# Sums written into the chain's operand and seeded into PSUM, in a fused network with three recurrences

## The reference, cut to what matters

```python
h = tanh(x_t @ Wx + h @ Wh + b)                     # stage 1, "rnn"
# then a selective state-space stage (mamba)
fused = sigmoid(concat([x_t, h]) @ w_W + w_b)       # stage 3, "gru"
hidden, output = split(fused, 2)
m = x_t @ wx_W + wx_b + hidden * (h @ wh_W + wh_b)
h = output * h + (1 - output) * tanh(m)
# then a feed-forward and a gated linear attention stage
a = x_t @ Wx + b + h @ Wh                           # stage 6, "lstm"
i, f, o, g = sigmoid, sigmoid, sigmoid, tanh of the quarters of a
c = f * c + i * g;  h = o * tanh(c)
# then a mixture of experts
```

## Time and profile before

| | |
|---|---|
| three runs | 8898.45, 8900.65, 8903.1 us; median 8900.65 |
| profiled execution | 8898.33 us, its span 8896.5 us |
| busy in the span | PE 70%, DVE 85%, ACT 48%, POOL 15% |
| rnn, from about 240 to 5419 us | DVE 4979.54 us busy of 5179 |
| GRU, about 7552 to 7952 us | DVE 143.17 us busy of 400 |
| LSTM, about 8258 to 8631 us | DVE 108.83 us busy of 373 |

### The profile page before, as it was taken

The page is one execution under the profiler, slowest core; times in us unless marked ns, Lnnn a source line. Parts: engine busy times, 40 slices in busy tenths (PEclk is TensorE's granted clock), DMA queues, the critical chain, the costliest instruction groups (busy, mean ns, idle before and its releaser), DMA issues. The chain is left out here.

```text
span 8896.5 us, 108600 instructions
## 1 busy us (share of the span) xinstructions
PE 6269.1 (70%) x33921; PEld 2486.1 (28%) x34193; DVE 7600.0 (85%) x12570; ACT 4291.4 (48%) x4428; POOL 1329.7 (15%) x1111
## 2 busy tenths in 40 slices
PE   5677777676767676767676764488888887662779
PEld 1222222222222222222222221122222222331443
DVE  5999999999999999999999996899999997336223
ACT  3666666665656665656665663233333332112222
POOL 0000000000000000000000000377777774000000
PEclk8888888888888888888888887799999999995999
DMA  0000000000000000000000000000000000000000
GB/s 6 1 1 1 1 1 1 1 1 1 1 1 1 1 1 1 1 1 1 1 1 1 1 1 22 17 3 4 4 4 4 4 4 3 0 6 3 3 14 5
DMA packets 14002, 27.97 MB, mean 3 GB/s; under 512 B 3665, under 2 KB 11602, under 8 KB 12434
## 3 DMA queue, kind: packets, MB, share of 16 engines
q1 hardware_dynamic: 13586, 22.47, 0.9%
HBM read 15.12 MB, written 7.34 MB: 3 GB/s over the span
## 5 line engine op out<-in xcount | busy, mean ns | idle before, releaser
L901 POOL TENSOR_TENSOR hc<-hh,cg 128x512 f32<-128x512 f32 x1024 | 1296.2, 1268 | 506.9 <-DVE hh L884 506.9
L829 ACT ACTIVATE ps_m<-ps_m,aneg 128x508 f32<-128x508 f32 x1024 | 673.4, 658 | 1188.6 <-DVE hh L884 1063.5
L884 DVE TENSOR_TENSOR_SCAN hh<-ps_m,bx 128x512 f32<-128x512 f32 x1024 | 1232.9, 1209 | 0.0
L800 PE MATMUL ps_m<-hc,pick 128*128 128x512 f32 x2048 | 1051.1, 597 | 2.1 <-POOL hc L901 0.8
L508 DVE TENSOR_TENSOR_SCAN co<-rx_d 128x772 f32<-128x772 f32 x544 | 915.4, 1745 | 0.0
L508 DVE TENSOR_TENSOR_SCAN co<-rh_d 128x3088 f32<-128x3088 f32 x128 | 843.8, 6592 | 31.8 <-ACT rh_d L366 28.6
L263 PE MATMUL r_ps<-rh_diag,whq 32*128 32x512 bf16 x3072 | 360.1, 624 | 666.9 <-DVE rh_diag L127 611.5
L866 DVE TENSOR_TENSOR bx<-ps_m,bg 128x512 f32<-128x512 f32 x1024 | 675.3, 664 | 45.9 <-PE ps_m L813 45.8
L439 POOL TENSOR_TENSOR r_gate<-ident 128x1 f32<-128x1 f32 x16 | 5.7, 356 | 4576.1 <-PE r_ps L255 4576.1
L255 PE MATMUL r_ps<-wdiag,xsp 32*128 32x512 bf16 x3312 | 311.4, 528 | 517.8 <-DVE rh_gain L171 186.4
L274 PE MATMUL r_ps<-rh_diag,whn 32*128 32x512 bf16 x4608 | 438.5, 548 | 267.9 <-ACT rh_pd L395 267.9
(11 more groups left out here) (389 smaller groups left out, 11206.2 us busy)
## 6 DMA issues: line engine op xcount, KB each, us to landing
rows_scratch<-pc SPq DMA_DIRECT2D x48, 128.0 KB
rows<-rows_scratch SPq DMA_DIRECT2D x128, 48.0 KB
ew<-in_e SPq DMA_DIRECT2D x3, 1024.0 KB, 6.8
co<-in_x_dn SPq DMA_DIRECT2D x1, 1024.0 KB, 4.8
xcur<-in_x_dn SPq DMA_DIRECT2D x1, 1024.0 KB
out_x<-xcur SPq DMA_DIRECT2D x1, 1024.0 KB, 3.9
qi<-in_f_q SPq DMA_DIRECT2D x1, 384.0 KB, 3.1
xpw<-in_xp_t SPq DMA_DIRECT2D x1, 257.0 KB
```

The costliest lines, as they stand in the source:

```text
L800: e.matmul(ps[:, 6, :], pick[:, 128 - un:256 - un], hc[un % NHC][:], start=False, stop=True, skip_group_check=True).then_inc(summed, 1)
L829: e.activation(da[un % NDA][:, :, 1:T], ps[:, un % 2, :].rearrange("p (n t) -> p n t", n=NG4)[:, :, 1:T], ACT.Exp, scale=aneg[:, 0:1]).the ...
L884: e.tensor_tensor_scan(hh[un % NBUF][:], da[un % NDA].rearrange("p n t -> p (n t)"), bx[un % NBUF][:], 0.0, ALU.mult, ALU.add).then_inc(sc ...
L901: e.tensor_tensor(hc[un % NHC][:], hh[un % NBUF][:], cg[:], ALU.mult).then_inc(weighted, 1)
```

## The change

It has three parts.

**The rnn's state half.** The tile `rh_s` is gone: DVE's odd scan and even addition write the sums straight into their places in `rh_d`, 12 bytes apart, and the even addition and the differences read them there. ACT no longer copies the sums. In its place it writes their negative into PSUM banks 4 to 7, in two instructions (odd and even), ahead of `rh_sg`, and TensorE no longer multiplies `negid` by the sums: its first matmul there adds the differences onto what ACT wrote. To make room for a place at the row's start, LX grows from 193 to 195, for X as well, so the chain scans get two elements longer for each of the 16 sequences. X keeps its own `rx_s`, its copy and its `negid` matmuls.

**The diagonals.** The identity is held ready in bf16 and repeated (`idn`), and each piece of h is stored twice side by side, so that all operands of L127 are bf16 with pairs of neighbours.

**The gates.** In GRU and LSTM DVE copies the input's part for step t + 1 into the other half of PSUM ahead of time, and PE adds the product with h onto it. ACT takes the sigmoids and the tanh straight from PSUM. In the GRU, `1 - update` is a third sigmoid (scale -1), `h * update` is formed beside the tanh, and two dependent operations stand behind the tanh, not three. PE's order is reset gate, candidate, update gate, and it gets three signals, not one. In the LSTM the first two gates are signalled ahead of the others. `WARM` goes from 6 to 5 in both.

```diff
-LX = 1 + 3 * NP
+LX = 3 * (1 + NP)
...
             def diagonal(q):
-                return tl.inc(e.tensor_tensor(F["diag"][:, q], id32[:].unsqueeze(1).to_broadcast([128, N, KB]),
-                                              F["part"][:, q, :].unsqueeze(2).to_broadcast([128, N, KB]), ALU.mult))
+                return tl.inc(e.tensor_tensor(halves(F["diag"][:, q]), halves(idn[:]),
+                                              F["part"][:, q].unsqueeze(2).to_broadcast([128, N, KB // 2, 2]), ALU.mult))
...
-                    remainder(4, R, h_stat, h_mov, (v, KV * t + V0 + 2), (v, KV * t + V0 + 3), h_diff, False)
-                    sticky(4, (ra, KA * t + NB + 2))
+                    onto_sums(4, (ra, KA * t + NB + 2), (v, KV * t + V0 + 3))
+                    sticky(4, (ra, KA * t + NB + 4))
...
+            def onto_sums(bank0, seeded, differenced):
+                e.wait_ge(*seeded)
+                e.wait_ge(*differenced)
+                for b in range(NB):
+                    e.matmul(ps[:, bank0 + b, :], ident[:], R["gain"][:, :, KB * b:KB * (b + 1)], start=False, stop=False,
+                             skip_group_check=True)
...
+                    e.wait_ge(v, KV * t + V0 + 2)
+                    e.wait_ge(xa, 5 * g + 1)
+                    for odd in range(2):
+                        e.activation(remainder_sums(4, 0, NB, odd), R["at"][:, :, odd, 4::3].rearrange("p n (b k) -> p n b k", b=NB),
+                                     ACT.Copy, scale=-1.0).then_inc(ra, 1)
                     e.wait_ge(rl_mm, t + 1)
                     e.activation(R["sg"][:, 0], ps[:, 0:4, :], ACT.Sign).then_inc(ra, 1)
                     e.activation(R["sg"][:, 1], ps[:, 0:4, :], ACT.Tanh, scale=1.0 / LEAST).then_inc(ra, 1)
-                    e.wait_ge(v, KV * t + V0 + 2)
-                    put_sums(R, ra)
...
+            def h_prefix_odd():
+                return prefix_odd(R, R["d"][:, 1, 2::3])
+            def h_prefix_even():
+                return e.tensor_tensor(R["at"][:, :, 0, 4::3], R["at"][:, :, 1, 1:LX - 3:3], R["pd"][:, :, 2:K2:2], ALU.add)
+            def h_difference():
+                return e.tensor_tensor(pairs(R["gain"][:]), R["at"][:, :, :, 4::3], pairs(R["pd"][:, :, 2:K2]), ALU.subtract)
...
-WARM = 6
+WARM = 5
...
+                        e.wait_ge(prod, t * KP + 1)
+                        e.activation(reset[:], ps[:, at, 0:N], ACT.Sigmoid).then_inc(act, 1)
+                        e.wait_ge(prod, t * KP + 3)
+                        e.activation(upd[:], ps[:, at + 1, 0:N], ACT.Sigmoid).then_inc(act, 1)
+                        e.activation(new[:], ps[:, at + 1, 0:N], ACT.Sigmoid, scale=-1.0).then_inc(act, 1)
+                        e.wait_ge(vec, t * KV + V0 + 2)
                         e.activation(th[:], r2[:], ACT.Tanh).then_inc(act, 1)
...
+                def seed(t, at):
+                    e.tensor_copy(ps[:, at:at + 2, 0:N], gxt[:, 0:2, bass.ds(t, 1), :].rearrange("p q a n -> p q (a n)")).then_inc(vec, 1)
...
-                        e.activation(s3[:], gate[:, 0:3, :], ACT.Sigmoid).then_inc(act, 1)
-                        e.activation(gg[:], gate[:, 3, :], ACT.Tanh).then_inc(act, 1)
+                        e.wait_ge(prod, t * KP + 1)
+                        e.activation(keeps[:].rearrange("p a n -> p (a n)"), ps[:, at, 0:2 * N], ACT.Sigmoid).then_inc(act, 1)
+                        e.wait_ge(prod, t * KP + 2)
+                        e.activation(gg[:], ps[:, at + 1, N:2 * N], ACT.Tanh).then_inc(act, 1)
+                        e.activation(out_[:], ps[:, at + 1, 0:N], ACT.Sigmoid).then_inc(act, 1)
```

More of the change, by code:

```diff
@@ L74, in rnn @@
         R, X = side("rh_"), side("rx_")
-        R.update(part=sb("rh_part", [128, 3, N], BF16), rest=sb("rh_rest", [128, 2, N]),
+        X.update(s=sb("rx_s", [128, N, K2]))
+        R.update(part=sb("rh_part", [128, 3, N, 2], BF16), rest=sb("rh_rest", [128, 2, N]),
                  diag=sb("rh_diag", [128, 3, N, KB], BF16), gain=sb("rh_gain", [128, N, D]),
@@ L112, in rnn @@
         V0 = 1
-        VSETUP = 57
+        VSETUP = 62
         class Tally:
@@ L137, in pieces @@
                 tl.wait(j)
-                i = tl.inc(e.tensor_tensor(F["part"][:, q, :], F["rest"][:, q - 1, :], nought[:], ALU.add))
+                i = cast(q, F["rest"][:, q - 1, :])
             tl.wait(i)
@@ L276, in residue, with remainder @@
                 return ins
-            def remainder(bank0, F, stat, mov, prefixed, differenced, diff, last):
+            def remainder(bank0, F, stat, mov, prefixed, differenced):
                 e.wait_ge(*prefixed)
@@ L283, in remainder @@
                 for b in range(NB):
-                    e.matmul(ps[:, bank0 + b, :], ident[:], diff(b), start=False, stop=False)
+                    e.matmul(ps[:, bank0 + b, :], ident[:], piece(F, "pd", b), start=False, stop=False)
                 for i, (q, r) in enumerate(LARGE_FIRST):
                     for b in range(NB):
-                        ins = e.matmul(ps[:, bank0 + b, :], stat(b, q), mov(b, r), start=False, stop=(last and i == 8))
+                        ins = e.matmul(ps[:, bank0 + b, :], stat(b, q), mov(b, r), start=False, stop=(i == 8))
                 return ins
+            def onto_sums(bank0, seeded, differenced):
[4 more added lines that the diff above has]
+                             skip_group_check=True)
+                for i, (q, r) in enumerate(LARGE_FIRST):
+                    for b in range(NB):
+                        e.matmul(ps[:, bank0 + b, :], h_stat(b, q), h_mov(b, r), start=False, stop=False, skip_group_check=True)
             def sticky(bank0, signed):
@@ L966, in gru @@
         gw = sb("gw", [128, 2, 2 * D]); gwx = sb("gwx", [128, D]); gwh = sb("gwh", [128, D]); gb = sb("gb", [128, 4])
-        gx = sb("gx", [128, 3, COLS])
-        gate = sb("gate", [128, 2, N]); sg = sb("sg", [128, 2, N]); r1 = sb("r1", [128, N]); r2 = sb("r2", [128, N])
-        th = sb("th", [128, N]); r3 = sb("r3", [128, N]); r4 = sb("r4", [128, N])
+        gx = sb("gx", [128, 3, COLS + N])
+        reset = sb("reset", [128, N]); upd = sb("upd", [128, N]); new = sb("new", [128, N])
+        r1 = sb("r1", [128, N]); r2 = sb("r2", [128, N]); th = sb("th", [128, N]); old = sb("old", [128, N]); r4 = sb("r4", [128, N])
         idle = sb("g_idle", [128, 512], BF16)
@@ L1011, in _ @@
                         t = STEPS * block + step
[L1012 to L1014 removed]
+                        at = 3 * (step % 2)
+                        e.wait_ge(prod, t * KP + 1)
[4 more added lines that the diff above has]
+                        e.wait_ge(vec, t * KV + V0 + 2)
                         e.activation(th[:], r2[:], ACT.Tanh).then_inc(act, 1)
```

155 lines of the change are left out of this document (85 added, 70 removed).

## The result

The changed kernel takes 9115.55 us (median of four, 9106.56 to 9117.1), the kernel before 8901.88 us beside it (8898.45 to 8903.94): a ratio of 1.0238, 95% interval 1.0226 to 1.0249. The change costs 2.4%. Its profiled execution has a span of 9104.7 us.

What follows compares the result with a forecast made beforehand. DVE bounds the rnn step, with PE and ACT only just in time; GRU and LSTM are chains of short operations. Rnn +141, GRU -111, LSTM -52 and setup +2 give -20 us: 8881 us, range 8750 to 9010.

Steps and rivals of the forecast that it cites:

- `WARM` 5 for 6: In GRU and LSTM, one zero matmul fewer a step; they run while PE has nothing to do, so no term.
- cold start: In the rnn, PE's `ident` group runs at low clock behind a 3.3 us pause: 0 to 3.1 us, taken as 2.0.
- The gates' work: Shorter chains in GRU and LSTM: GRU wins 0.87 us a step, 111 us; LSTM 0.41 us a step, 52 us.
- Rival (d): In the gates, DVE's added copy and address computations make its product late: half the gain, 8959 us; chance 0.08.
- The rnn's sum: PE bounds the rnn; the mean step grows from 40.30 to 41.40 us, and 128 steps lose 141 us.
- differences: DVE's 2048-element operation in the rnn, now reading sums 12 bytes apart: 3.04 us instead of 2.29.
- ACT's pair: ACT's two writes of negated sums to PSUM in the rnn: 3.1 us together, bounds 2.1 and 4.3.
- The first step of a turn: One rnn step in eight: its start comes 2.35 us later, less 0.35 of waiting that goes, so 2.0.
- The diagonals: Three DVE products in each rnn step: 0.43 us each instead of 0.68; of 0.77 us saved, some 0.4 counts.
- (a): Strides paid, cold start partly; rnn loses 100 to 185 us, gates win 150 to 175: 8825 to 8930; chance 0.45.
- (b): In the rnn, strides are cheap or DVE's bound holds: rnn within 60 us of before, 8765 us; chance 0.23.
- (c): In the rnn, full cold start or ACT's pair over 3.4 us: mean step from 41.7 us, 9019 us; chance 0.24.

Runs made afterwards that it cites:

- e2: The kernel before with five zero matmuls in each GRU and LSTM step instead of six: 9080.7 us, ratio 1.0205 to before.
- e1: The changed kernel with six zero matmuls in each GRU and LSTM step instead of five: 8857.9 us, ratio 0.9958 to before.
- e6: The kernel before with the changed GRU and LSTM, six zero matmuls a step there, and the rnn's 16-bit diagonals: 8648.9 us, ratio 0.9727 to before.
- e3: The kernel before with the changed GRU and LSTM and six zero matmuls a step there, rnn untouched: 8711.5 us, ratio 0.9789 to before.
- e7: As e6, but ACT seeds PSUM in one operation with negated sums that DVE writes side by side: 8718.7 us, ratio 0.9801 to before.
- e10: As e6, with seven zero matmuls in each GRU and LSTM step instead of six: 8656.4 us, ratio 0.9717 to before.
- e11: As e6, with no zero matmuls in the GRU and LSTM steps: 8808.0 us, ratio 0.9891 to before.
- e5: As e1, with 22 zero matmuls behind the rnn's residue product, in PE's pause: 8808.7 us, ratio 0.9900 to before.
- e8: As e7, with 16 zero matmuls behind the rnn's residue product: 8816.7 us, ratio 0.9911 to before.
- e9: As e1, without ACT's seeds: PE negates the sums itself, reading them from `rh_d`: 9040.0 us, ratio 1.0147 to before.
- e4: As e1, with 13 zero matmuls behind the rnn's residue product, in PE's pause: 8806.8 us, ratio 0.9896 to before.

## Why the prediction was wrong, point by point

**The step that failed** is this: "`WARM` 5 for 6: the zeros' matmuls run while PE has nothing to do, and one less keeps the shorter step free of them; no term." The trace of before had the fillers and a granted clock of 1.00 together, and I read the fillers as idle work only. They held the clock: with five the granted clock is 0.50 to 0.52 over both loops (e2, and the changed kernel once it has fallen), with six 1.00 (e1). e2 prices the one filler in the old kernel at 9080.7 - 8894.1 = 187 us, e1 in the new one at 9115.6 - 8857.9 = 258 us. In the prediction every cold start was looked for in the rnn, and no rival had one in the gates.

**The gates' work** was under-estimated. With the clock held (e1) GRU gains 400.0 - 285.2 = 115 us for 111, and LSTM 372.3 - 304.4 = 68 for 52. In LSTM the tanh of g starts 1.10 us behind PE's first record (8401.60 - 8400.50), where it started 1.59 behind (8377.47 - 8375.88), which is 0.49 us of the 0.53 gained; the prediction had 0.41. Rival (d), a late product behind the seed, did not come.

**The rnn's sum** held: 41.36 us a step for 41.40, 136 us for 141, and its terms too: even sums 1.56 for 1.60, differences 2.95 for 3.04, ACT's pair 3.07 for 3.1, start of `ident` 13.11 for 13.1, its group 5.39 for 3.60 + 2.0, DVE's wait ahead of the long scan 0.71 for about 1. The first step of a turn came 3.1 us longer than the others, for 2.0, and the common one 40.9 for 41.15; the two errors cancel. The diagonals gave 0.49 to 0.61 us, for 0.4 (e6).

**Three readings in the rnn's sum were off.** The differences don't change in their reads of the sums alone: with the change L530 also steps through `rh_pd` and `rh_gain` at 8 bytes, so its 0.66 us more are not the price of the 12-byte read by itself. The pause ahead of PE's group wasn't new either. In 27 of the 127 steps before, the residue ran at the full clock and took 2.12 us, and in most of them PE paused for 1.5 to 1.7 us, at no cost:

```profile
656.51 3.70 PE L281 MATMUL r_ps<-rh_s,negid 128*128 128x512 f32 x8 [1.68 <-DVE rh_s L501]
```

And the granted clock in `ident` was 0.68, not 0.50.

**Which part costs what**, by steps: the diagonals 39.67 - 40.28 = -0.61 us (e6, e3), the seeds with their pause 40.21 - 39.67 = +0.54 (e7, e6), the strides 41.36 - 40.21 = +1.15 (e1, e7), together +1.08. The same rnn took 39.67, 39.83 and 39.72 us in the profiled executions of e6, e10 and e11, so each share is good to some 0.2. That the longer `ident` group is the pause's work is shown by e5 and e8, in which it takes 3.6 to 3.7 us once PE has next to no pause. That the pause is the whole of the seeds' +0.54 is not shown, for both of these runs lost elsewhere what the group gave back. The strides' share is only that difference, and no run has the strides alone: in it are 0.33 + 0.66 us more on DVE for even sums and differences, the longer chains (0.14 in the prediction), ACT's pair at 3.07 us for one seed at 1.88, and the copy of the sums that ACT no longer makes.

**The rivals.** (a) would have come true with six fillers: 8881 / 8900.65 = 0.9978 was forecast, and e1 has 0.9958. (b) needed cheap strides; even sums and differences took 1.56 and 2.95 us, about what L189's price gives. (c) gives 9019 us and has the sign of the result, but not its reason: the mean step is 41.36 us, under its point of 41.7.

**The rule of the Trainium skill** (TensorE: Matmul & The Clock Gate, HAM oscillation) was given its full price of 3.1 us in one sentence of the prediction, and 2.0 in the sum; the changed kernel shows 1.8 us in common steps and up to 2.5 in the others. "Each time anew" holds there, but not in every kernel: in e7 24 of 127 groups took 3.7 us behind their pause. The same page says (Part 1: The HAM clock gate) that the low clock is the default and activity lifts it. By that rule idle matmuls may be what holds the clock, and the prediction did not weigh that. The rows agree in part: the granted clock is 1.00 with six and seven and 0.50 to 0.52 with five and none, but with five PE's records filled 354.00 us of 354.00 and the clock was not lifted.

**What stays open.** Why five are too few and six enough is not settled. PE's busy share does not tell it: GRU before held the full clock with PE busy 270.07 us of 400 and the changed one lost it at 33.46 of 40. What fixes the price of a pause is open as well: in the kernel before, the `negid` group at 2957.34 us took 5.77 us behind a pause of 0.88, and the one at 656.51 took 3.70 behind 1.68. Nor was it tried whether fewer, or narrower, fillers at another place in the step would do.

## What to carry to other kernels

Idle matmuls in a loop of short dependent steps can hold TensorE's clock and are then no spare work: change their number and the step's length in separate runs, and look at the granted clock of the whole loop, not of its first steps. Here five were worse than none (GRU steps of 3.23 us for 2.63), because at the low clock they stood on the path. And a group of matmuls that is dropped from ahead of a wait leaves a pause, and the next group may pay the pause back at half clock; here PE's dropped work (3.7 us) gave nothing.

## What the runs showed of the hardware that was not expected

- TensorE reads its moving operand more slowly when neighbours are far apart: 6.61 us for eight fp32 records of 512 columns whose elements come by turns from two halves of a tile, some 12 KB apart, 3.70 us side by side, both at the full clock (e9, e6). The Trainium skill (Advanced Engine Details and Errata, SBUF Cachelines) asks for two hits on a line of 16 bytes and names a penalty without a size; here no two successive reads share a line, and the trace agrees and gives 1.8 times.
- At the low clock PE had records without a gap (354.00 us busy of 354.00) and the granted clock still did not rise for the rest of the loop, in GRU and in LSTM.
- In a timeline one row can hide a change of clock: the residue takes 2.12 us at a granted clock of 1.00 (e4, from 3080.91 us) and 4.03 at 0.50 (e5, from 3042.86 us), and between two steps of one kernel it is now the one and now the other.
- bf16 on all operands, with pairs of neighbours, took DVE's 512-element product from 0.68 to 0.42 us.
